# One block for the first attention and the first gated stage: where the gated stage's preparation is placed

## The reference, cut to what matters

```python
# attention: 16 heads of width 128, 64 slots each
x = x + _L0_attn_ref(_L0_cond_ref(x, ...), Wq, Wk, Wv, Wg, Wo, ...)
# gated stage with low-rank adapters chosen per sequence, then a ternary feed-forward
gate = x @ Wg + (x @ Ag[id]) @ Bg[id]          # 256 -> 1024, rank 16
up   = x @ Wu + (x @ Au[id]) @ Bu[id]
h    = silu(gate) * up
z    = h @ Wd + (h @ Ad[id]) @ Bd[id]          # 1024 -> 256
w1q, w3q, w2q = ternary(w1), ternary(w3), ternary(w2)   # clip(round(w/s), -1, 1) * s, s = mean|w|
x = x + (silu(z @ w1q.T) * (z @ w3q.T)) @ w2q.T         # 256 -> 682 -> 256
```

## Time and profile before

| | us |
|---|---|
| median of 3 runs (1452.36 to 1455.73) | 1453.72 |
| the profiled execution | 1453.34 |
| its span, first to last instruction | 1451.2 |
| mean granted TensorE clock, share of full speed | 0.966 |
| PE busy, share of the span | 92% |
| DVE busy, share of the span | 65% |
| POOL busy, share of the span | 38% |
| ACT busy, share of the span | 36% |

### The profile page before, as it was taken

One profiled execution on the slowest core, in us unless ns is written; L12 is line 12 of the kernel. 1 busy time (PEld: TensorE's weight loads), 2 busy tenths in 40 slices (PEclk: granted clock), 3 DMA queues, 4 the chain that ended last, 5 costly groups with the idle time before them and its releaser, 6 DMA issues. The chain is left out here.

```text
span 1451.2 us, 36830 instructions
## 1 busy us (share of the span) xinstructions
PE 1329.9 (92%) x14806; PEld 1063.4 (73%) x14806; DVE 938.1 (65%) x1825; ACT 516.8 (36%) x1188; POOL 556.4 (38%) x608
## 2 busy tenths in 40 slices
PE   4999999999999999999985889999997789997997
PEld 3788888888888888888763667778776567775665
DVE  3787888878788778878764474252524245666786
ACT  2344444444444444444443213231322122222433
POOL 1656565565656556555532212121221111122111
PEclk9999999999999999999997899999999789997998
DMA  6000000000000000000003400000000720000620
GB/s 194 5 13 13 16 13 12 27 13 17 12 13 27 17 13 13 1 2 2 1 2 116 144 1 1 1 0 0 0 0 0 223 75 0 0 0 13 197 63 22
DMA packets 33375, 46.46 MB, mean 32 GB/s; under 512 B 6974, under 2 KB 22552, under 8 KB 32728
## 3 DMA queue, kind: packets, MB, share of 16 engines
q1 hardware_dynamic: 30888, 43.81, 9.9%
q10 hardware_dynamic: 2272, 0.52, 0.2%
q0 software_dynamic: 80, 0.26, 0.1%
HBM read 42.22 MB, written 2.36 MB: 31 GB/s over the span
## 5 line engine op out<-in xcount | busy, mean ns | idle before, releaser
L425 PE MATMUL OE<-w_o,ogT_s 128*128 128x256 f32 x512 | 137.9, 392 | 0.7 <-ACT ogT_s L513 0.7
L890 POOL TENSOR_TENSOR hT_lo<-h,hT_hi 128x512 fp32r<-128x512 f32 x44 | 56.8, 1291 | 192.6 <-ACT hT_hi L1063 192.6
L239 POOL TENSOR_TENSOR turned<-t1c,t2s 128x512 f32<-128x512 f32 x62 | 78.7, 1269 | 123.6 <-DVE t2s L650 123.6
L675 DVE RECIPROCAL enz<-SC 128x128 f32<-128x128 f32 x128 | 121.2, 947 | 0.4
L1126 DVE SCALAR_TENSOR_TENSOR t<-th,m 128x512 f32<-128x512 f32 (+1 forms) x56 | 38.4, 685 | 121.2 <-ACT th L1068 93.4
L280 POOL TENSOR_TENSOR exz<-ex,enz 128x256 f32<-128x256 f32 x64 | 47.4, 741 | 159.9 <-ACT ex L583 159.9
L324 PE MATMUL PJ<-hs_hi,w_hi 128*128 128x512 f32 x248 | 102.6, 414 | 0.0
L335 PE MATMUL PJ<-w_hi,hs_hi 128*128 128x512 f32 x256 | 101.0, 394 | 0.0
L335 PE MATMUL PJ<-w_hi,hs_lo 128*128 128x512 f32 x256 | 100.6, 393 | 0.0
L335 PE MATMUL PJ<-w_lo,hs_hi 128*128 128x512 f32 x256 | 100.5, 393 | 0.0
L324 PE MATMUL PJ<-hs_hi,w_lo 128*128 128x512 f32 x248 | 97.2, 392 | 0.0
(11 more groups left out here) (381 smaller groups left out, 3572.0 us busy)
## 6 DMA issues: line engine op xcount, KB each, us to landing
we_ring<-in_we SPq DMA_DIRECT2D x64, 256.0 KB, 3.1
w_raw<-in_w_slices SPq DMA_DIRECT2D x48, 128.0 KB, 2.1
xres<-in_x SPq DMA_DIRECT2D x2, 1024.0 KB, 8.6
turned<-in_w_slices SPq DMA_DIRECT2D x4, 512.0 KB, 4.5
out_rows<-xres SPq DMA_DIRECT2D x16, 128.0 KB, 1.7
w1r<-in_w1i SPq DMA_DIRECT2D x1, 1408.0 KB, 6.7
w_s<-in_w SPq DMA_DIRECT2D x2, 682.0 KB
w_o<-in_wo SPq DMA_DIRECT2D x1, 1024.0 KB, 5.7
```

The lines of the kernel that those rows point to most:

```text
L239: pool.tensor_tensor(to[:, 0, :], x1c[:, :], x2s[:, :], ALU.subtract)
L425: m = pe.matmul(OE[:, SW:SW + D], ogT_s[:, i % 2, h * P:(h + 1) * P], w_o[:, i // G % 2, h, :], start=(h == 0), stop=(h == HQ - 1))
L675: dve.reciprocal(enz[:, cols], SC[:, SW:2 * SW][:, cols]).then_inc(z_rec, 1)
L890: eng.tensor_tensor(hT[1][s, m % 2, :], h[s, m % 2, :], hT[0][s, m % 2, :].bitcast(F32), ALU.subtract).then_inc(second, 1)
```

## The change

`attention0` and `mlp0` become one block, `layer0`, in which `mlp0` gives each engine a function `early(i, ...)` that is called at fixed places of the attention's loop, and a `main()` that is called after it. What was ahead of the first slab's `gates` is put into the attention's steps 58 to 63, on all engines:

- PE, in the places of `x1` and `x2`: step 58 the 8 transposes of the first slab (straight from `xres`, rows that the last quarter has finished), step 59 `rank` (12), steps 60, 61 and 62 gates 0, 1 and 2 (18 each). After the loop gates 3 stand between `heads_out(62)` and `turn_og(63)`, gates 4 ahead of `heads_out(63)`, and then come `down(0)`, `down(1)`, gates 5, `down(2)`, the sum of the ternary sizes, gates 6, `down(3)`, gates 7, `down(4)` to `down(7)`.
- The gate and up weights are 16 more slices (n = 64 to 79) of the slice queue; they are split in the steps 47 to 62 into the slot that quarter 2 has left. `bg` and `bu` go into the q and k columns of the other slot in steps 58 to 60, `wd` into the columns behind them.
- ACT, DVE and POOL get the matching splits, masks, tanh and `gated` calls at the beginning, behind `ogT_out`, or at the end of their iterations 55 to 63.
- The ternary weights are loaded when `wd` has been split and the last `turn_og` is done; `prepare` moves to m = 4 to 7 (sizes after `gated(4)`, `t1` after 5, `t3` after 6, `t2` after 7). `following` is loaded after the ternary work.
- Many tiles move: `xT`, `hT`, `u` and the adapters' parts lie in `hs_hi` and `hs_lo`, the raw weights in one buffer `raw` that also holds `t1c` to `t2s`, `v_s`, `gs` and the masks of the attention.
- `renew()` now stands between `mlp0` and `attention1` and no longer between `attention0` and `mlp0`. One load (`ada_i`) joins those that the attention's start waits for (`ld`), and the first `w_o` load is issued as two.

The slabs 1 to 3 keep their instructions.

```diff
+            early, main = nxt.sync(sp)
...
-            for n in range(LEAD, STEPS):
+            for n in range(LEAD, STEPS + G):
+                early(n)
...
                 if j < TURNS:
                     rotate(j)
-                if now and LEAD + i < STEPS:
+                else:
+                    early(i)
+                if now and LEAD + i < STEPS + G:
                     split(LEAD + i)
...
                     quarter(j, 0, x1_mm)
+                elif j < TURNS + FIRST:
+                    pe.wait_ge(v_ev, j - FIRST + 1)
+                    early(j - FIRST - 1, 0)
...
             heads_out(LAST - 1)
+            gates(3)
             turn_og(LAST)
+            gates(4)
             heads_out(LAST)
+            main()
...
                 if now:
                     pT_out(i)
+                    early(i, 0)
                 if i >= 1:
                     ogT_out(i - 1)
+                    early(i, 1)
...
                 if now:
+                    early(i, 0)
                     mask_weights(i)
...
             y_out(LAST - 1)
+            gated_ahead(3)
             y_out(LAST)
+            main()
...
+    def sync(sp):
+        def early(n):
+            if n == STEPS + 6:
+                sp.wait_ge(at.y_mm, ONE)
+                sp.dma_start(a_raw[:, 0:KD * P], flat(ag)).then_inc(a_in, 16)
+                sp.dma_start(a_raw[:, KD * P:2 * KD * P], flat(au)).then_inc(a_in, 16)
+            if n == STEPS + 12:
+                sp.wait_ge(at.qk_add, STEPS)
+                sp.dma_start(b_raw[:, 0:F], bg).then_inc(b_in, 16)
+                sp.dma_start(b_raw[:, F:2 * F], bu).then_inc(b_in, 16)
+
+        def main():
+            sp.wait_ge(a_second, 1)
+            sp.dma_start(a_raw[:, :], flat(ad)).then_inc(d_in, 16)
+            sp.wait_ge(at.a_mm, STEPS - 4)
+            sp.dma_start(bd_raw, bd).then_inc(d_in, 16)
+            sp.wait_ge(b_second, 2)
+            sp.dma_start(wd_raw, flat(wd)).then_inc(wd_in, 16)
+            sp.wait_ge(wd_second, 1)
+            sp.wait_ge(at.ogT_tr, STEPS)
...
+    def gpsimd(pool):
...
+        def early(i):
+            n = i - STEPS
+            if n == -6:
+                b_low(0)
+            if n == -5:
+                b_low(1)
+                u_low(0)
+            if n in (-4, -3):
+                h_low(pool, n + 5, n + 4, slice(0, P), h_first, h_second)
...
+    def tensor(pe):
...
+        def early(i, part):
+            n = i - STEPS
+            if n == -6:
+                turn_first(part)
+            elif n == -5:
+                rank_first(part)
+            elif n == -4:
+                gate_part(0, part, 0)
+                if part == 1:
+                    pe.wait_ge(b_second, 2)
+                    pe.wait_ge(u_second, 1)
+                    bias_part(0, 0, 0)
+                    bias_part(0, 1, 0)
+            elif n in (-3, -2):
+                gate_part(n + 4, part, 0)
+                bias_part(n + 4, part, 0)
...
+                down(0, 0)
+                down(0, 1)
+                for m in range(EARLY, FC):
+                    gates_first(m)
+                    down(0, m - EARLY + 2)
+                    if m == EARLY:
+                        pe.wait_ge(ones_set, 2)
+                        pe.wait_ge(tern_abs, 1)
+                        pe.wait_ge(at.y_add, STEPS)
+                        pe.matmul(bank[7][:, 0:4], ones[:, :], sums, start=True, stop=True).then_inc(tern_sum, 1)
+                for m in range(FC - EARLY + 2, FC):
+                    down(0, m)
...
+    def scalar(act):
...
+            if (n, place) == (-9, 2):
+                a_high()
+            elif (n, place) == (-5, 0):
+                xT_first_half(0)
+                xT_first_half(1)
+            elif n == -5:
+                b_high(place - 1)
+            elif (n, place) == (-4, 1):
+                u_high(0)
+            elif n >= -3 and place == 0:
+                gate_tanh(0, n + 3, 0)
+            elif n in (-3, -2) and place == 1:
+                first_high(n + 3)
+            elif (n, place) == (-1, 2):
+                d_high()
...
+    def vector(dve):
...
+            if (n, place) == (-6, 1):
+                a_low()
+                one_hot()
+            elif (n, place) == (-5, 0):
+                x_low_first(0)
+                x_low_first(1)
+            elif (n, place) == (-4, 0):
+                choose_first()
+            elif n >= -3 and place == 0:
+                gated_first(n + 3)
+            elif (n, place) == (-1, 1):
+                d_low()
...
+            if m == 4:
+                sizes()
+            elif m == 5:
+                scales()
+            elif m == 6:
+                ternary(t3[:, :, :], w3_s, 4)
+            elif m == 7:
+                ternary(t2[:, 0:full, :], w2_s[:, 0:full, :], 5)
+                ternary(t2[0:hw[-1], full, :], w2_s[0:hw[-1], full, :], 5, hw[-1]).then_inc(tern_done, 1)
...
+        lasting = [(k.ident, a["identity"]), (k.pcol, a["pcol"]), (k.prow, a["prow"]), (ada_i, a["ada0"].partition_broadcast(P))]
+        layer0(nc, k, xres, raw, ada_i, lasting, loads1, [a[n] for n in MLP0], *[a[n] for n in ATT0])
         renew()
```

More of the change, by code:

```diff
@@ new lines, in mlp0, with take, in_two @@
+    ONE = G * (NQ - 1)
+    EARLY = 5
+    sb, _, sem = k.tools(ctx)
+    a_raw = sb("a_raw", [P, FC * P])
+    work = sb("work", [P, 8 * W])
+    at_col = [0]
+    def take(width):
+        at_col[0] += width
+        return work[:, at_col[0] - width:at_col[0]]
+    def in_two(ap):
+        return ap.rearrange("p (a b) -> p a b", a=2)
+    th, t, h, ugm, uum = in_two(take(2 * W)), take(W), in_two(take(2 * W)), take(W), take(W)
+    bd_raw, idx_f, hot, sums, scl = take(D), take(B), take(B), take(4), take(12)
@@ new lines, in mlp0, with flat, first_bank, h_low @@
+    tern_in, tern_abs, tern_sum, tern_done = [sem("m0_tern_" + n) for n in "in abs sum done".split()]
+    f_tanh, f_t, f_h, f_first, f_second, f_dn, h1_mm, h3_mm = [sem("m0_" + n) for n in (
+        "f_tanh f_t f_h f_first f_second f_dn h1_mm h3_mm").split()]
+    def flat(ap):
+        return ap if len(ap.shape) == 2 else ap.rearrange("p a b -> p (a b)")
+    def first_bank(m):
+        return 0 if m < 3 else m % 2
+    def h_low(eng, n, m, s, first, second):
+        eng.wait_ge(first, n)
+        eng.tensor_tensor(hT[1][s, m % 2, :], h[s, m % 2, :], hT[0][s, m % 2, :].bitcast(F32),
+                          ALU.subtract).then_inc(second, 1)
@@ L1030, in step @@
[L1030 to L1038 removed]
+            if nxt:
+                turn(i + 1)
+            pe.wait_ge(ad_second, i + 1)
+            for c in range(KD):
+                m = product(bank[4 + c][:, :], [b[:, c * P:(c + 1) * P] for b in bd_p], adm_p, False, True)
+            m.then_inc(z_mm, 1)
@@ new lines, in step @@
+            if nxt:
+                rank(i + 1)
+            pe.wait_ge(z_second, i + 1)
+            if first:
+                pe.wait_ge(tern_done, 1)
+            for m in range(HC):
+                cols = slice(m * P, m * P + hw[m])
+                if m >= 2:
+                    pe.wait_ge(f_h, i * HC + m - 1)
+                for n, (a, done) in enumerate(((t1, h1_mm), (t3, h3_mm))):
+                    if nxt and m < 2 and n == 1:
+                        pe.wait_ge([ug_mask, u_mask][m], i + 2)
+                    for c in range(KD):
+                        for j in range(2):
+                            q = pe.matmul(bank[2 * n + m % 2][0:hw[m], :], a[:, c, cols], zT[j][:, c, :],
+                                          start=(c == 0 and j == 0), stop=(c == KD - 1 and j == 1))
+                    q.then_inc(done, 1)
+                if m >= 2:
+                    fdown(i, m - 2)
@@ L1039, in _, with main @@
+            fdown(i, HC - 2)
+            if nxt:
+                gates(i + 1, 0)
+            fdown(i, HC - 1)
+        def main():
             step(0)
```

810 lines of the change are left out of this document (413 added, 397 removed).

## The result

The changed kernel takes 1407.15 us (median of 4 runs, 1407.07 to 1409.49) beside 1453.38 before: 0.9684 of the time, interval 0.9667 to 0.9700, so it is faster by 46.2 us where 36.3 were forecast; 1407.15 lies 2.9 us under the range's low end. Run once more beside other kernels, unedited, it gave 0.9701 (0.9682 to 0.9721), 43.6 us. The two profiled executions (spans 1451.2 and 1405.4) differ by 45.8.

The account below looks back on a forecast made before the run. TensorE's work was taken as the bound, with chain waits in late steps and boundary, loads and slow clock in the first slab. +10.5 - 48.4 + 1.25 + 0.3 = -36.3 us gave 1417.4 us; range 1410 to 1427.

Parts of the forecast that it names:

- Steps 58 to 62: The attention's last steps, carrying the moved work as fillers: 60.35 us instead of 49.84, so +10.5 us.
- 0.5 us for `exz` in step 60: Allowance for POOL reaching `exz(61)` late behind `b_low(1)` and `u_low`: nothing to 1 us, taken as 0.5.
- 0.3 for the gated pair in step 61: Allowance for DVE's gated pair ahead of `mask_weights`, making `slot_scores` late by 0.3 us.
- rival 4: In the attention, `b_high(0)` waits for a late `bg` and `bu` load, stopping all engines; likely 2 to 5 us; chance 0.03.
- step 63 to `down(7)`: From the attention's end through the first slab: 46.4 us instead of 94.8, so -48.4 us.
- The chain's length: DVE's ternary work in the first slab, from the first step on `scl` to the end of `t2`: 19.76 us.
- The pause: TensorE's wait ahead of `down(7)` in the first slab, with DVE the bound: 4.0 us.
- Rival 2: The first slab's ternary work on DVE is hidden, 4.0 us and part of the slow start go: 1411 to 1412; chance 0.11.
- Rival 1: POOL and DVE delay each other: 1 us in each of six steps, 3 in the ternary chain, 1426; chance 0.16.
- What follows `down(7)` in slab 0: The rest of the first slab was taken as unchanged in time.
- if slabs 1 to 3 change their length: Sign that the forecast is wrong: the later slabs were given no change in time.
- the barrier's +1.25: The boundary from `mlp0` to `attention1`, now with `renew()`, grows by 1.25 us from 0.29.

Follow-up runs that it names:

- a_sizes: Changed kernel with the ternary sizes between the two halves of `gated(4)` instead of behind it: 0.9686 of before, 1406.69 us without one outlying execution.
- a_t2late: Changed kernel with the ternary `t2` in parts behind `h_low(7)` and TensorE's wait for it moved to the first ternary down product: 0.9683 of before, 1405.72 us.
- a_last: Changed kernel with `t2` behind `h_low(7)`, its last six instructions together behind zT's remainder: 0.9671 of before, 1403.72 us.
- b_aligned: Kernel before with 32 unused bytes in a partition ahead of the first slab's `x_st`: 0.9979 of before.
- a_apart: Changed kernel with 32 unused bytes between `hs_lo` and `w_hi`: 0.9757 of before, 1418.1 us.
- the gaps: Changed kernel with 64, 128 or 256 unused bytes between `hs_lo` and `w_hi`: 0.9752, 0.9749 and 0.9696 of before.
- b_banks: Kernel before with the first gated stage's eight PSUM banks in the physical order that the changed kernel uses: 0.9994 of before.
- b_att1: Kernel before with 32 unused bytes ahead of the second attention's own tiles: 1.0002 of before.
- a_again: Changed kernel run once more, unedited: 1408.84 us, 0.9701 of before.
- a_aligned: Changed kernel with 32 unused bytes ahead of `hs_hi`, so `hs` and the weights start at a multiple of 64: 0.9699 of before, 1409.0 us.
- a_gap256: Changed kernel with 256 unused bytes between `hs_lo` and `w_hi`: 0.9696 of before.
- a_att1: Changed kernel with 96 unused bytes ahead of the second attention's tiles: 0.9708 of before.
- a_uT: Changed kernel with the tile `uT` (8192 bytes in a partition) between `hs_lo` and `w_hi` instead of behind `turned`: 0.9688 of before.

## Why the forecast was right, and where it was wrong

**Right: what bounds the kernel, and the change's own steps.** Steps 58 to 62 took 10.28, 11.74, 12.66, 12.66 and 12.28 us (forecast 10.15, 11.5, 13.2, 13.0 and 12.5). The fillers cost what the sum says, TensorE's work beyond the idle time of the late steps; of the two delays that I added by judgement (0.5 us for `exz` in step 60, 0.3 for the gated pair in step 61) neither came, and steps 60 to 62 have no idle time at all. The loads were hidden: nothing waited for `bg` and `bu`, so rival 4 (slower) did not happen, and the ternary load landed at about 790.8 in a_sizes, where DVE waited 0.44 us for it: 18.8 us after that run's step 63, for 19.2.

**Right mechanism, size off: step 63 to `down(7)`.** 47.95 us for 46.4. The chain's length was right by 0.1 us. Its start was 1.8 us late, for two reasons. TensorE's `down(2)` was done 1.2 us late: I put each `heads_out` at 0.9 us, and the two took 1.6 and 1.5 (775.95 to 777.59 and 786.46 to 788.00), so `down(0)` began 16.3 us after step 63 and not 15.05. The other 0.6 us are `gated(4)`, of which I did not ask what it waits for: its half of `h` is freed by POOL's `h_low(2)`, that by ACT's `h_high(2)`, and that by `down(0)`; a_sizes got 0.6 us back there and no more. The pause (3.59 us) came out nearly right because TensorE was late as well. a_t2late and a_last show that VectorE is the bound here, as the step says, and that some 3 us were to be had (2.8 and 3.4 in their traces). Rival 2, the hidden chain, did not happen, though the time lies below its 1411 to 1412: the pause was there, and what brought the time down lies elsewhere.

**Rival 1**, the shared port, did not come as forecast (6 us in the steps, 3 in the chain), but it is in the trace: DVE's `L1363` took 1.96 us at 802.38, beside a `h_low` of POOL, and the same instruction 0.87 us in a_sizes, where POOL's came 0.4 us later; there the one behind it took 2.54 instead of 1.58. Two such delays of 1.1 us stand in the chain. They cost nothing against the forecast, since the 19.76 us of the earlier trace rows held the like. The Trainium skill, "SBUF — State Buffer", section "Who interferes with whom", names both kinds, a DVE instruction with two SBUF inputs and a `tensor_scalar` in a faster mode; the traces agree for both (1.0 and 1.1 us longer).

**Wrong: that code which keeps its instructions keeps its time.** The prediction says it of slab 0 ("What follows `down(7)` in slab 0 keeps its instructions and follows a TensorE pause of about the same length (4.0 against 3.64 us), so I take it as unchanged"), and by the same reason its sum has no term for the slabs 1 to 3 and, but for the boundary, none for the second attention. This is the step that failed. It had named the sign itself: "if slabs 1 to 3 change their length". The runs show three things in its place.

- Slabs 1 to 3: -3.1 us. The change puts weights and moving tiles into other places, and b_aligned, a_apart and the gaps show that this alone moves a 512-column matmul of the gated stage from 0.2333 to 0.2276 us, 1.1 to 1.2 us a slab. I had read the 0.233 in the earlier trace rows as the price of the matmul and not asked why the attention's own matmuls start 0.227 apart. The Trainium skill, "TensorE: Matmul & The Clock Gate", section "Wait — 56ns, not 53.3ns?", gives 215.7 ns for warm 512-column matmuls back to back; no stretch here comes that low.
- Behind `down(7)`: -1.2 us, and this is not placement: b_aligned takes 34.64 us there, like the kernel before, and a_apart 33.64, like the changed one. The pause was as long as forecast, but the clock behind it was 0.92 before and 0.95 after. In stretches of 4 us it was 0.50 and 0.81 from 860 us on before, and 0.60 and 1.00 from 820 us on after. TensorE had worked without a long pause until then in the changed kernel; that this is the reason is not shown.

```profile
859.96:894.63 34.67, 32.33 (x150) 25.38 (x151) 15.38 (x24) 11.80 (x20) 7.70 (x6) 0.92 0.00 1
```

- The second attention: 3 us shorter, where the forecast has only the barrier's +1.25. The barrier itself costs 1.36 us, so that term was right. Whether it also brings the shorter form of the attention is open.

**Wrong as a method: one execution as the base.** The start (-3.6 us against the forecast; the first residual add at 87.1 before and at 83.1 after) is chance, and the 0.7 us of the steps 0 to 57 go the other way: over five executions with the old start the first residual add came at 82.1 to 87.1 us (mean 84.5), over thirteen with the new one at 82.8 to 86.5 (mean 84.4), and the profiled execution that I summed against had the latest. Elsewhere it was lucky: from step 61 to slab 0's residual add it took 125.2 us, three others with the same instructions 126.9, 127.3 and 127.6. Over three profiled executions of the old kernel (before, b_banks, b_att1) and six of the new one with the pitch of 0.2276 (the changed kernel, a_again, a_aligned, a_gap256, a_att1, a_uT) the mean spans differ by 44.6 us: start 0.0, from there to step 61 +9.3, to slab 0's residual add -48.4, slabs -3.1, boundary and second attention -2.6, the rest +0.1. Against this the forecast of 36.3 misses 8.3 us, nearly all of it in the failed step: 3.1, 1.2, and 3.9 for the second attention. The forecast's range reached 7.4 us down, for a hidden chain and cheaper steps, and not for any of these.

## What to carry to other kernels

When a change moves tiles, the untouched code that reads them is not untouched: compare the pitch of its matmuls, in a long run without waits, in two stages of the same kernel, before taking one of them as the price. Date every operand of a chain's first instruction by its own releaser, the buffer's too. And take the base of a sum of small terms from several executions; here one alone was 1.6 to 3.2 us off the mean of the others in three different places.

## What the runs showed of the hardware that I had not expected

A float32r matmul of 512 columns started 0.2276 us after the one before where weights and moving tile begin at the same place in a block of 256 bytes, and 0.2326 to 0.2334 where they differ by 32, 64 or 128: seven placements of `hs` and the weights in the changed kernel and two in the kernel before agree with that. That holds for the gated stage. The ternary stage keeps 0.2314 with equal starts, and the attention's projections are at 0.2295 with equal starts in the changed kernel and at 0.2271 in the kernel before, so the rule is not complete.
